# GpSimd adds the second norm's bias to the residual, and makes its dbx products two columns at a time

## The chip, the cores and the metric

The kernel runs on one core of one Trainium2 chip. The core has five engines with queues of their own: TensorE (PE) multiplies matrices into PSUM, VectorE (DVE) and ScalarE (ACT) do elementwise work, GpSimd (POOL) does elementwise work on SBUF, and SyncE (SP) issues the DMAs. The engines meet only at semaphores. The metric is device time of one launch in microseconds; lower is better.

## The reference, cut to what matters

The layer takes x of shape 4 x 2048 x 256 in f32. It is a Mamba block followed by an RWKV channel mix, each with a layernorm ahead of it and a residual around it:

```python
x = x + L0_attn_ref(layernorm(x), ...)
x = x + L0_ffn_ref(layernorm(x), ...)

# L0_attn_ref, N = 16 states for each of the 256 channels
dA  = exp(delta[..., None] * A)                  # b l d n
dBx = (delta * x)[..., None] * B_ssm[:, :, None] # b l d n
h   = dA_t * h + dBx_t                           # over l, for each d and n
y_t = sum over n of h[d, n] * C_t[n]
y   = y + x * D_param
res = (y * silu(z)) @ W_out + x_in
return (res - mean) * rsqrt(var + eps) * ln_g + ln_b
```

The sum that the channel mix starts from is therefore x + (normed res) * ln_g + ln_b. The term ln_b, a vector of 256 numbers that is the same for every token, is the bias that the change is about. The channel mix is r * ((relu(k) ^ 2) @ W_v^T), with r and k made from a mix of each token with the one before it.

## The kernel before, in words

The work is cut into 16 chunks of 512 tokens, four to a batch. A chunk of data with channels on the partitions is 2 halves x 512 tokens, that is 128 x 1024 numbers; with tokens on the partitions it is 4 blocks x 256 channels, also 128 x 1024.

For each chunk there are 16 columns, one per state n. A column takes these steps:

- ACT makes dA in PSUM, one activation per half (`exps`, line 662).
- POOL makes dbx = u * B_n in SBUF (`times_b`, line 543). u is delta * x of the chunk, B_n one row of the ring `b_ring`, spread over all partitions by a DMA. The result goes to the ring `dbx`, which has X_RING = 4 places.
- DVE runs the recurrence as a scan, one per half (`scans`, line 1045), into PSUM or into the ring `hg` of 8 places.
- The product with C_n, a row of the ring `c_ring`, is made either by DVE out of PSUM (the columns of SPLITS, lines 1052 and 1061) or by POOL in place in `hg` (the other, "whole" columns, `times_c`, line 556). Of the 16 columns, 8 or 9 are DVE's, by chunk parity; in the last chunk only 6.
- PE adds the product to y by transposes into PSUM (`add_up`, line 1331). This waits for POOL's product (semaphore g_pool) or DVE's (g_vec).

The order on each engine is written out by hand. A step t of the program has 16 places n (32 half-places on ACT and DVE). In place n, POOL makes the dbx product of column n + B_LEAD (3 before), then the C product of column n - C_LAG (1). PE adds up column n - Y_LAG (2). Tables such as PE_TURN and ACT_TURN say in which place each piece of dense work runs, so that step t works on the scan of chunk t, prepares chunk t + 1, and finishes chunks t - 1 (gate, W_out, second norm, residual) and t - 2 (channel mix). Each engine does its instructions strictly in this order, so one that waits holds up all that stand behind it.

The dbx product of column n waits for the scans of column n - 4, whose place it takes. `load_b` and `load_c` on SP fill the rings `b_ring` and `c_ring`, two groups of four rows each: a group is loaded once all products of the group two before it are made. SP's DMAs are in one queue too.

The second norm's result stands in a PSUM bank (`wo0`, `wo1`). DVE scales it (`affine`, line 1074). Then PE adds on top of it, in the loop `xa`, the residual `xres` by matmuls with the identity (line 1479) and the bias by transposes of `b_wide` (line 1485), where `b_wide` holds the bias of a channel in every column. ACT reads the bank back to `xres` with a running sum (`sum3`, line 880).

Of the kernel before, what the change touches and what calls it, by code (L numbers as in the profile page):

```python
# [5 lines left out]
P = 128  # L6
BATCH, LEN, D = 4, 2048, 256
NS = 16
LC = 512
# [8 lines left out]
X_RING = 4  # L18
# [6 lines left out]
B_LEAD, C_LAG, Y_LAG = 3, 1, 2  # L25
# [23 lines left out]
POOL_TURN = dict(nr1=13)  # L49
# [47 lines left out]
def mamba_rwkv_layer(nc, x_in, W_in, W_x, W_dt, b_dt, A_log, D_param, W_out, ln_g, ln_b,  # L97
# [12 lines left out]
    with ExitStack() as ctx:  # L110
# [6 lines left out]
        def sem(name):  # L117
# [22 lines left out]
        b_wide = sb("b_wide", P, KH, P)  # L140
# [66 lines left out]
            w_out_set b_set  # L207
# [157 lines left out]
        def c_of(n):  # L365
            return c_ring[:, n // GN % BG, n % GN:n % GN + 1, :]
# [48 lines left out]
        def _(sp):  # L415
# [33 lines left out]
            def step(t, par, pre=False, scan=False, mid=False, end=False, late=False, more=False):  # L449
# [3 lines left out]
                if scan:  # L453
                    if not (t == 0):
                        load_c(t, 1)
# [3 lines left out]
                if scan:  # L459
                    load_b(t, 2)  # L460
                    load_c(t, 2)
                    load_b(t, 3)
# [5 lines left out]
                if scan:  # L468
                    load_c(t, 3)
                if pre:  # L470
# [6 lines left out]
                    if start:  # L477
                        load_c(0, 1, True)
# [23 lines left out]
        def _(pool):  # L502
# [23 lines left out]
            def times_b(i, ip, n):  # L526
# [16 lines left out]
                pool.tensor_tensor(dbx[:, n % X_RING, :, :], u[:, ip, :, :], b.to_broadcast([P, KH, LC]),  # L543
                                   ALU.mult).then_inc(s["dbx_done"], 1)

            def times_c(i, n):

                need(pool, c_loaded[n // GN], 16 * (i + 1))
                if i == 0 and n == 0:
                    pool.wait_ge(s["w_loaded"], 16 * W_LOADS)  # L550
                if ends(i):
                    need(pool, s["scan_done"], KH * (NS * i + n + 1))
                else:
                    need(pool, s["carry_saved"], kept_wholes(i, n))
                part = hg[:, n % H_RING, :, :]
                pool.tensor_tensor(part, part, c_of(n).to_broadcast([P, KH, LC]), ALU.mult).then_inc(s["g_pool"], 1)  # L556
# [6 lines left out]
            def step(t, par, pre=False, scan=False, mid=False, end=False, late=False, more=False):  # L563
                nxt = 1 - par
                for n in range(NS):
                    if more and t >= 0 and n == POOL_TURN["nr1"]:
                        scale_mean(t + 3)
                    ahead = column_at(t, par, n + B_LEAD, scan, pre, mid)
                    if ahead:
                        times_b(*ahead)  # L570
                    behind = column_at(t, par, n - C_LAG, scan, pre, mid)
                    if behind and behind[2] in whole_of(behind[0]):
                        times_c(behind[0], behind[2])
                    if late and n == NS - 1:
                        for m in range(NS - C_LAG, NS - 1):
# [1049 lines left out]
```

## Time and profile before

| what | value |
|---|---|
| median of 3 runs | 941.3 us (941.04 to 941.36) |
| the profiled execution, its own time | 941.56 us |
| its span, first to last instruction | 939.8 us |
| mean granted TensorE clock | 0.978 |
| DVE busy | 900.5 us (96%) |
| POOL busy | 890.4 us (95%) |
| PE busy | 858.4 us (91%) |
| ACT busy | 837.5 us (89%) |

Some 1.8 us of the profiled execution lie outside the span. The busy shares are means over the whole span, which has a start of some 24 us and an end of some 27 us in which POOL has next to nothing to do. Busy times add up instruction durations as the profiler has them; two neighbours on POOL overlap there by some hundredths of a microsecond, so the distance from one start to the next is the better measure of what an instruction costs its engine.

### The profile page before, as it was taken

What the parts mean: (1) busy time and instruction counts of PE and PEld (TensorE: products, weight loads), DVE (VectorE), ACT (ScalarE), POOL (GpSimd) and SP (SyncE); (2) the same over time, 40 slices, a digit from 0 to 9 for tenths busy, and PEclk for the clock granted to TensorE, in tenths of its full rate; (3) what the DMA queues carried; (4) which work ended last, traced back from release to release, by engine and by line L of the source; (5) the groups of instructions that cost most, each with busy time, mean ns of one, the idle gap of its engine ahead of it and who ended that gap; (6) DMA issues with size and microseconds to landing.
All of it is one profiled execution on the core that took longest, in us unless ns stands there. A gap on an engine that the chain in (4) does not pass through costs nothing.

```text
span 939.8 us, 15796 instructions
## 1 busy us (share of the span) xinstructions
PE 858.4 (91%) x5024; PEld 685.0 (73%) x5024; DVE 900.5 (96%) x986; ACT 837.5 (89%) x2007; POOL 890.4 (95%) x413
## 2 busy tenths in 40 slices
PE   8766679989999898989999898998999899899998
PEld 5545466867878586776868678786878768678876
DVE  5899999999999999999999999999999999999896
ACT  4776889999999999998999999998999999978875
POOL 4999999999999999999999999999999999999980
PEclk9977899999999999999999999999999999999999
DMA  7345435462644644454374634446354454445231
GB/s 229 149 179 204 180 135 205 180 242 103 226 157 156 225 178 159 183 190 181 150 248 156 224 140 174 166 179 248 144 194 182 144 195 180 157 161 224 90 103 45
DMA packets 49939, 163.60 MB, mean 174 GB/s; under 512 B 5249, under 2 KB 33153, under 8 KB 33601
## 3 DMA queue, kind: packets, MB, share of 16 engines
q1 hardware_dynamic: 48528, 161.27, 46.0%
q0 software_dynamic: 512, 1.31, 0.5%
q8 instruction: 40, 0.66, 0.3%
q14 instruction: 43, 0.34, 0.1%
q10 hardware_dynamic: 816, 0.02, 0.1%
HBM read 153.15 MB, written 9.44 MB: 173 GB/s over the span
## 4 chain that ended last, share of the span: by engine, by line
PE 40%; ACT 27%; DVE 20%; issue 11%; POOL 1%; POOLq 0%; DVEq 0%; ACTq 0%
PE w_ps L1340 9%; ACT da_ps L662 9%; PE y_ps L1331 8%; DVE da_ps L1045 7%; PE w_ps L1364 5%; DVE hg L1045 4%; PE w_ps L1373 4%; PE w_ps L1376 4%; DVE hg L1052 4%; DVE hg L1061 3%; PE w_ps L1479 2%; ACT h_tok L599 2%; ACT zs L723 2%; PE w_ps L1382 2%; ACT xn_tok L599 2%
## 5 line engine op out<-in xcount | busy, mean ns | idle before, releaser
L543 POOL TENSOR_TENSOR dbx<-u,b_ring 128x1024 f32<-128x1024 f32 x255 | 599.7, 2379 | 2.0 <-DVE hg L1045 1.9
L662 ACT ACTIVATE da_ps<-delta,a_neg 128x512 f32<-128x512 f32 x512 | 340.2, 684 | 25.9 <-DVE hg L1052 8.6
L556 POOL TENSOR_TENSOR hg<-hg,c_ring 128x1024 f32<-128x1024 f32 x122 | 290.2, 2379 | 7.5 <-ACT carry L668 6.7
L1331 PE MATMUL y_ps<-ident,hg 128*128 128x128 f32 x2048 | 261.8, 278 | 10.4 <-POOL hg L556 10.2
L1331 PEld LDWEIGHTS y_ps<-ident,hg 128*128 128x128 f32 x2048 | 239.9, 144 | 37.4 <-issue 17.8
L1045 DVE TENSOR_TENSOR_SCAN da_ps<-da_ps,carry,dbx 128x512 f32<-128x512 f32 x203 | 249.5, 1270 | 3.5 <-ACT da_ps L662 3.5
L1045 DVE TENSOR_TENSOR_SCAN hg<-da_ps,carry,dbx 128x512 f32<-128x512 f32 x181 | 220.3, 1264 | 2.1 <-ACT carry L668 1.7
L1052 DVE TENSOR_TENSOR hg<-da_ps,c_ring 128x1024 f32<-128x1024 f32 x68 | 82.3, 1210 | 0.2
L1061 DVE TENSOR_TENSOR hg<-da_ps,c_ring 128x512 f32<-128x512 f32 x130 | 82.3, 673 | 0.0
L1045 DVE TENSOR_TENSOR_SCAN da_ps<-da_ps,dbx 128x512 f32<-128x512 f32 x64 | 75.4, 1211 | 3.4 <-ACT da_ps L662 3.1
L1045 DVE TENSOR_TENSOR_SCAN hg<-da_ps,dbx 128x512 f32<-128x512 f32 x64 | 74.8, 1206 | 2.4 <-ACT da_ps L662 2.4
L1340 PE MATMUL w_ps<-xnT_ring,w_in 128*128 128x512 f32 x120 | 61.7, 638 | 16.0 <-ACT xT L704 14.1
L1373 PE MATMUL w_ps<-w_rT,mixed 128*128 128x256 f32 x240 | 61.7, 380 | 0.0
L1376 PE MATMUL w_ps<-w_r_prev,mixed 128*128 128x256 f32 x240 | 61.6, 379 | 0.0
L1364 PE MATMUL w_ps<-w_in,xnT_ring 128*128 128x256 f32 x248 | 59.4, 382 | 0.9 <-ACT delta L696 0.6
L1340 PE MATMUL w_ps<-xnT_ring,w_dtx 128*128 128x512 f32 x120 | 57.9, 606 | 0.9 <-ACT bc_rows L808 0.9
L1364 PE MATMUL w_ps<-w_out,gated 128*128 128x256 f32 x248 | 58.7, 379 | 0.0
L1340 PE MATMUL w_ps<-mixed,w_kT 128*128 128x512 f32 x120 | 57.3, 601 | 0.0
L1364 PEld LDWEIGHTS w_ps<-w_in,xnT_ring 128*128 128x128 f32 x248 | 45.5, 190 | 15.0 <-ACT kact L690 4.9
L1373 PEld LDWEIGHTS w_ps<-w_rT,mixed 128*128 128x128 f32 x240 | 44.4, 190 | 11.4 <-issue 6.7
L1364 PE MATMUL w_ps<-w_vT,kact 128*128 128x256 f32 x232 | 52.6, 379 | 0.0
L1376 PEld LDWEIGHTS w_ps<-w_r_prev,mixed 128*128 128x128 f32 x240 | 45.6, 190 | 6.2
(214 smaller groups left out, 1320.7 us busy)
## 6 DMA issues: line engine op xcount, KB each, us to landing
c_ring<-bc_rows_dram SPq DMA_DIRECT2D x64, 1024.0 KB, 4.6
b_ring<-bc_rows_dram SPq DMA_DIRECT2D x63, 1024.0 KB, 6.6
xres<-in_L_attn_x_in_dram SPq DMA_DIRECT2D x16, 512.0 KB, 4.7
x_tok<-in_L_attn_x_in_dram SPq DMA_DIRECT2D x15, 512.0 KB, 6.0
out_dram<-r_out SPq DMA_DIRECT2D x14, 512.0 KB, 3.2
bc_rows_dram<-bc_rows SPq DMA_DIRECT2D x64, 16.0 KB, 5.4
w_in<-in_L_attn_W_in_dram SPq DMA_DIRECT2D x2, 256.0 KB, 4.3
x_tok<-in_L_attn_x_in_dram SPq DMA_DIRECT2D x2, 256.0 KB, 4.6
```

What stands on the lines that cost most here:

```text
L543: pool.tensor_tensor(dbx[:, n % X_RING, :, :], u[:, ip, :, :], b.to_broadcast([P, KH, LC]), ALU.mult).then_inc(s["dbx_done"], 1)
L556: pool.tensor_tensor(part, part, c_of(n).to_broadcast([P, KH, LC]), ALU.mult).then_inc(s["g_pool"], 1)
L599: last = act.activation(dst[j], src[j], ACT.Identity, scale=rs[j], bias=nm[j])
L662: act.activation(da_of(n, h), delta[:, ip, h, :], ACT.Exp, scale=a_neg[:, h, n:n + 1]).then_inc(s["da_ready"], 1)
L1045: dve.tensor_tensor_scan(out, da_of(n, h), dbx[:, n % X_RING, h, :], 0.0 if first else carry[:, n, h:h + 1], ALU.mult, ALU.add).then_inc(s ...
L1052: dve.tensor_tensor(hg[:, n % H_RING, :, :], da_both(n), c_of(n).to_broadcast([P, KH, LC]), ALU.mult).then_inc(s["g_vec"], 1)
L1061: last = dve.tensor_tensor(hg[:, n % H_RING, h:h + 1, :], da_ps[:, at:at + 1, :], c_of(n), ALU.mult)
L1331: last = pe.matmul(y_tok[:, b, h * P:(h + 1) * P], hg[:, n % H_RING, h, b * P:(b + 1) * P], ident[:, :], is_transpose=True, start=n == 0 a ...
L1340: last = pe.matmul(out, w[:, k, cols], x[:, k, :], start=k == 0, stop=k == KH - 1)
L1364: last = pe.matmul(by_block(out)[:, b, :], xT_[:, k, tokens], w[:, k, :], start=b == 0 and k == 0 and not begun, stop=k == KH - 1, skip_gr ...
L1373: pe.matmul(by_block(out)[:, b, :], h_of[:, k, at_b + 1:at_b + 1 + P], w_rT[:, k, :], start=k == 0, stop=False)
L1376: last = pe.matmul(by_block(out)[:, b, :], h_of[:, k, at_b:at_b + P], w_r_prev[:, k, :], start=False, stop=k == KH - 1)
```

## The change

POOL gets a new instruction, `add_bias`, once in each of the steps 1 to 15, ahead of the other work of place 5: it adds the bias (`b_all`, the bias on every partition) to `xres` in place, 128 x 1024 numbers. PE waits for this (`xb_done`) in place of the DMA, does only its identity matmuls, and no longer the transposes of `b_wide`; `b_wide` and the two activations that fill it are gone. In the last chunk the bias was and is added by DVE.

The dbx products of two neighbouring columns are made by one instruction (`times_b_twice`), in the even places, except the first two columns of the program. For that X_RING is 6, B_LEAD is 4, and a pair waits for the scans of the column that stood in the second of its two places. C products go on one by one (C_RUN = 1 makes every run one column long). On SP the loads of B stand ahead of the loads of C that used to be in front of them.

```diff
-X_RING = 4
+X_RING = 6
+C_RUN = 1
-B_LEAD, C_LAG, Y_LAG = 3, 1, 2
+B_LEAD, C_LAG, Y_LAG = 4, 1, 2
-POOL_TURN = dict(nr1=13)
+POOL_TURN = dict(xb=5, nr1=13)
...
         @block.sync
                 if scan:
+                    load_b(t, 2)
                     if not (t == 0):
                         load_c(t, 1)
...
                 if scan:
-                    load_b(t, 2)
+                    load_b(t, 3)
                     load_c(t, 2)
-                    load_b(t, 3)
...
-                if scan:
-                    load_c(t, 3)
                 if pre:
                     need(sp, s["bc_stored"], 16 * TB * (t + 2))
...
                     load_b(t + 1, 0, start)
+                if scan:
+                    load_c(t, 3)
+                if pre:
+                    if not start:
+                        load_b(t + 1, 1)
                     load_c(t + 1, 0, start)
-                    load_b(t + 1, 1, start)
...
         @block.gpsimd
+            def times_b_twice(i, ip, n):
+
+                need(pool, b_loaded[n // GN], 16 * (i + 1))
+                for m in range(KH):
+                    need(pool, s[f"u{m}_done"], i + 1)
+                need(pool, s["scan_done"], KH * (NS * i + n + 1 - X_RING + 1))
+                at, row = dbx_of(i, n), n % GN
+                b = b_ring[:, n // GN % BG, row:row + 2, :]
+                pool.tensor_tensor(dbx[:, at:at + 2, :, :], u[:, ip, :, :].unsqueeze(1).to_broadcast([P, 2, KH, LC]),
+                                   b.unsqueeze(2).to_broadcast([P, 2, KH, LC]), ALU.mult).then_inc(s["dbx_done"], 2)
...
+            def add_bias(t, nxt):
+
+                need(pool, s["xres_loaded"], 16 * t)
...
+                part = xres[:, nxt, :, :]
+                pool.tensor_tensor(part, part, b_all[:, :].unsqueeze(1).to_broadcast([P, TB, D]), ALU.add).then_inc(s["xb_done"], 1)
...
                 for n in range(NS):
+                    if mid and n == POOL_TURN["xb"]:
+                        add_bias(t, nxt)
...
-                    if ahead:
+                    if ahead and ahead[0] == 0 and ahead[2] < HEAD_COLS:
                         times_b(*ahead)
+                    elif ahead and ahead[2] % 2 == 0:
+                        times_b_twice(*ahead)
...
         @block.tensor
-                            need(pe, s["xres_loaded"], 16 * t)
+                            need(pe, s["xb_done"], t)
...
                             for j in range(2):
-                                pe.matmul(b[:, j, :], ident[:, :], xres[:, nxt, 2 * v + j, :], start=False, stop=False,
-                                          skip_group_check=True)
-                            if t == 1:
-                                pe.wait_ge(s["b_set"], KH)
-                            for j in range(2):
-                                for k in range(KH):
-                                    last = pe.matmul(b[:, j, k * P:(k + 1) * P], b_wide[:, k, :], ident[:, :],
-                                                     is_transpose=True, start=False, stop=True, skip_group_check=True)
+                                last = pe.matmul(b[:, j, :], ident[:, :], xres[:, nxt, 2 * v + j, :], start=False, stop=True,
+                                                 skip_group_check=True)
```

How the rows move on POOL in the last chunk, before. L543 is a dbx product, L556 a C product, L584 the half C product of the last column; the names in brackets are the semaphores waited for:

```order
L543 TENSOR_TENSOR dbx<-u,b_ring 128x1024 [waits u1_done,scan_done,u0_done,b_loaded2] x3
L556 TENSOR_TENSOR hg<-hg,c_ring 128x1024 [waits scan_done,c_loaded1]
L543 TENSOR_TENSOR dbx<-u,b_ring 128x1024 [waits u1_done,scan_done,u0_done,b_loaded3] x3
L556 TENSOR_TENSOR hg<-hg,c_ring 128x1024 [waits scan_done,c_loaded2]
L543 TENSOR_TENSOR dbx<-u,b_ring 128x1024 [waits u1_done,scan_done,u0_done,b_loaded3]
L556 TENSOR_TENSOR hg<-hg,c_ring 128x1024 [waits scan_done,c_loaded3] x2
L584 TENSOR_TENSOR hg<-hg,c_ring 128x512 [waits scan_done,c_loaded3]
```

And the same place now, where L572 is a pair of dbx products, L587 a C product, L596 the bias, L625 the half product:

```order
L596 TENSOR_TENSOR xres<-xres,b_all 128x1024 [waits xres_loaded]
L587 TENSOR_TENSOR hg<-hg,c_ring 128x1024 [waits scan_done,c_loaded1]
L572 TENSOR_TENSOR dbx<-u,b_ring 128x2048 [waits u1_done,u0_done,scan_done,b_loaded2]
L572 TENSOR_TENSOR dbx<-u,b_ring 128x2048 [waits u1_done,u0_done,scan_done,b_loaded3]
L587 TENSOR_TENSOR hg<-hg,c_ring 128x1024 [waits scan_done,c_loaded1]
L572 TENSOR_TENSOR dbx<-u,b_ring 128x2048 [waits u1_done,u0_done,scan_done,b_loaded3]
L587 TENSOR_TENSOR hg<-hg,c_ring 128x1024 [waits scan_done,c_loaded2]
L587 TENSOR_TENSOR hg<-hg,c_ring 128x1024 [waits scan_done,c_loaded3] x2
L625 TENSOR_TENSOR hg<-hg,c_ring 128x512 [waits scan_done,c_loaded3]
```

The last dbx products (columns 14 and 15) have moved ahead of the C product of column 10 (the one with c_loaded2), which had only the dbx product of column 15 behind it before.

On PE, a place of a middle step where the residual and the bias go on top of the second norm, before (L1331 is `add_up`, L1500 adds x * D to y):

```order
L1331 MATMUL y_ps<-ident,hg 128x128 x16
L1479 MATMUL w_ps<-xres,ident 128x256 x2
L1485 MATMUL w_ps<-ident,b_wide 128x128 x4
L1479 MATMUL w_ps<-xres,ident 128x256 x2
L1485 MATMUL w_ps<-ident,b_wide 128x128 x4
L1331 MATMUL y_ps<-ident,hg 128x128 x8
L1500 MATMUL y_ps<-ident,xT 128x128 x8
```

And now (L1368 is `add_up`, L1516 the residual, L1531 x * D):

```order
L1368 MATMUL y_ps<-ident,hg 128x128 x16
L1516 MATMUL w_ps<-xres,ident 128x256 x4
L1368 MATMUL y_ps<-ident,hg 128x128 x8
L1531 MATMUL y_ps<-ident,xT 128x128 x8
```

The eight transposes of a step are gone, and nothing else on PE has changed its place.

On SP, the DMAs of one middle step before, from the load of the residual to the store of the output:

```order
L452 DMA xres<-in_L_attn_x_in_dram 128x4x256
L446 DMA c_ring<-bc_rows_dram 128x2048 [waits g_pool,g_vec]
L458 DMA x_tok<-in_L_attn_x_in_dram 128x4x256 [waits xn_done]
L437 DMA b_ring<-bc_rows_dram 128x2048 [waits dbx_done]
L446 DMA c_ring<-bc_rows_dram 128x2048 [waits g_pool,g_vec]
L437 DMA b_ring<-bc_rows_dram 128x2048 [waits dbx_done]
L466 DMA bc_rows_dram<-bc_rows 32x128 [waits bc_rows_done]
L466 DMA bc_rows_dram<-bc_rows 32x128 x3
L446 DMA c_ring<-bc_rows_dram 128x2048 [waits g_pool,g_vec]
L437 DMA b_ring<-bc_rows_dram 128x2048 [waits dbx_done,bc_stored]
L446 DMA c_ring<-bc_rows_dram 128x2048 [waits g_pool,g_vec]
L437 DMA b_ring<-bc_rows_dram 128x2048 [waits dbx_done]
```

And now:

```order
L467 DMA xres<-in_L_attn_x_in_dram 128x4x256
L452 DMA b_ring<-bc_rows_dram 128x2048 [waits dbx_done]
L461 DMA c_ring<-bc_rows_dram 128x2048 [waits g_pool,g_vec]
L474 DMA x_tok<-in_L_attn_x_in_dram 128x4x256 [waits xn_done]
L452 DMA b_ring<-bc_rows_dram 128x2048 [waits dbx_done]
L461 DMA c_ring<-bc_rows_dram 128x2048 [waits g_pool,g_vec]
L481 DMA bc_rows_dram<-bc_rows 32x128 [waits bc_rows_done]
L481 DMA bc_rows_dram<-bc_rows 32x128 x3
L452 DMA b_ring<-bc_rows_dram 128x2048 [waits dbx_done,bc_stored]
L461 DMA c_ring<-bc_rows_dram 128x2048 [waits g_pool,g_vec]
L452 DMA b_ring<-bc_rows_dram 128x2048 [waits dbx_done]
L461 DMA c_ring<-bc_rows_dram 128x2048 [waits g_pool,g_vec]
```

Each B load now stands ahead of a C load that it stood behind.

## Rows read from the trace of the kernel before

**Rows 1.** The profile page, busy time by engine: us (share), instructions.

```profile
PE 858.4 (91%) x5024; PEld 685.0 (73%) x5024; DVE 900.5 (96%) x986; ACT 837.5 (89%) x2007; POOL 890.4 (95%) x413
```

**Rows 2.** The page, the chain that ended last, share by engine.

```profile
PE 40%; ACT 27%; DVE 20%; issue 11%; POOL 1%; POOLq 0%; DVEq 0%; ACTq 0%
```

**Rows 3.** Busy time by stretch: stretch, length, engines (instructions), clock, DMA.

```profile
400.00:460.00 60.00, 56.68 (x344) 45.56 (x343) 59.97 (x64) 55.94 (x135) 60.00 (x29) 1.00 0.52 193
520.00:580.00 60.00, 56.57 (x341) 45.45 (x340) 59.88 (x64) 56.93 (x141) 57.73 (x27) 1.00 0.45 168
40.00:880.00 840.00, 771.68 (x4562) 619.65 (x4562) 826.36 (x859) 772.20 (x1864) 831.30 (x372) 0.98 0.48 178
```

**Rows 4.** Waits of POOL: line, releaser, total us, times, longest.

```profile
POOL hg L556 <- ACT carry L668: 6.7, 9, 1.7
POOL dbx L543 <- DVE hg L1045: 1.9, 3, 0.9
POOL hg L556 <- DVE hg L1045: 0.8, 1, 0.8
```

**Rows 5.** Waits of DVE and of PE, in the same form.

```profile
DVE da_ps L1045 <- ACT da_ps L662: 6.6, 11, 1.4
DVE da_ps L1045 <- POOL dbx L541: 0.3, 1, 0.3
...
PE w_ps L1382 <- ACT xn_tok L599: 28.9, 14, 2.6
```

**Rows 6.** POOL's groups by shape: busy us, mean ns, idle before.

```profile
L543 POOL TENSOR_TENSOR dbx<-u,b_ring 128x1024 f32<-128x1024 f32 x255 | 599.7, 2379 | 2.0 <-DVE hg L1045 1.9
L556 POOL TENSOR_TENSOR hg<-hg,c_ring 128x1024 f32<-128x1024 f32 x122 | 290.2, 2379 | 7.5 <-ACT carry L668 6.7 <-DVE hg L1045 0.8
L561 POOL TENSOR_TENSOR nr<-nm,rs 128x4 f32<-128x4 f32 x14 | 3.0, 217 | 0.0
L584 POOL TENSOR_TENSOR hg<-hg,c_ring 128x512 f32<-128x512 f32 x1 | 1.3, 1272 | 0.0
```

**Rows 7.** POOL in order of time, the first products: start, us.

```profile
23.31 1.26 POOL L541 TENSOR_TENSOR dbx<-u,b_ring 128x512 f32<-128x512 f32 x1 [0.90 <-DVE u L1082]
24.54 11.63 POOL L543 TENSOR_TENSOR dbx<-u,b_ring 128x1024 f32<-128x1024 f32 x5
36.10 2.37 POOL L556 TENSOR_TENSOR hg<-hg,c_ring 128x1024 f32<-128x1024 f32 x1
```

**Rows 8.** POOL in order of time, the last products.

```profile
901.18 2.38 POOL L556 TENSOR_TENSOR hg<-hg,c_ring 128x1024 f32<-128x1024 f32 x1
903.50 2.38 POOL L543 TENSOR_TENSOR dbx<-u,b_ring 128x1024 f32<-128x1024 f32 x1
906.69 4.71 POOL L556 TENSOR_TENSOR hg<-hg,c_ring 128x1024 f32<-128x1024 f32 x2 [0.81 <-DVE hg L1045]
911.36 1.27 POOL L584 TENSOR_TENSOR hg<-hg,c_ring 128x512 f32<-128x512 f32 x1
```

**Rows 9.** PE in order of time, the same stretch.

```profile
904.15 1.04 PE L1331 MATMUL y_ps<-ident,hg 128*128 128x128 f32 x8
905.02 1.03 PE L1373 MATMUL w_ps<-w_rT,mixed 128*128 128x256 f32 x4
...
908.48 2.78 PE L1331 MATMUL y_ps<-ident,hg 128*128 128x128 f32 x24
911.10 0.60 PE L1357 MATMUL da_ps<-ident,xnT_ring 128*128 128x128 f32 x4
911.53 1.04 PE L1331 MATMUL y_ps<-ident,hg 128*128 128x128 f32 x8
912.77 1.06 PE L1331 MATMUL y_ps<-ident,hg 128*128 128x128 f32 x8 [0.21 <-POOL hg L584]
```

**Rows 10.** The chain from 340 to 400 us: start, us, piece.

```profile
345.80 0.44 PE w_ps L1485 x4
```

**Rows 11.** DMA issues: size of one, median us to landing.

```profile
c_ring<-bc_rows_dram SPq DMA_DIRECT2D x64, 1024.0 KB, 4.6
b_ring<-bc_rows_dram SPq DMA_DIRECT2D x63, 1024.0 KB, 6.6
```

More of the change, by code:

```diff
@@ L363, in column_at, with c_of, dbx_of, products_of @@
             return (t, par, n) if scan else None
-        def c_of(n):
-            return c_ring[:, n // GN % BG, n % GN:n % GN + 1, :]
+        def c_of(n, k=1):
+            return c_ring[:, n // GN % BG, n % GN:n % GN + k, :]
+        def dbx_of(i, n):
+            return (NS * i + n) % X_RING
+        def products_of(i):
+            runs = []
+            for n in whole_of(i):
+                if i == LAST and n == NS - 1:
+                    break
+                if runs and len(runs[-1]) < C_RUN and runs[-1][-1] == n - 1 and n % GN:
+                    runs[-1].append(n)
+                else:
+                    runs.append([n])
+            return runs
         def da_of(n, h):
@@ L542, in times_b, with times_c @@
                     return
-                pool.tensor_tensor(dbx[:, n % X_RING, :, :], u[:, ip, :, :], b.to_broadcast([P, KH, LC]),
+                pool.tensor_tensor(dbx[:, dbx_of(i, n), :, :], u[:, ip, :, :], b.to_broadcast([P, KH, LC]),
                                    ALU.mult).then_inc(s["dbx_done"], 1)
-            def times_c(i, n):
+            def times_b_twice(i, ip, n):
[7 more added lines that the diff above has]
+                                   b.unsqueeze(2).to_broadcast([P, 2, KH, LC]), ALU.mult).then_inc(s["dbx_done"], 2)
+            def times_c(i, run):
+                n, k = run[0], len(run)
                 need(pool, c_loaded[n // GN], 16 * (i + 1))
@@ L551, in times_c @@
                 if ends(i):
[L552 removed]
+                    need(pool, s["scan_done"], KH * (NS * i + run[-1] + 1))
                 else:
[L554 to L556 removed]
+                    need(pool, s["carry_saved"], kept_wholes(i, run[-1]))
+                slot = n % H_RING
+                part = hg[:, slot:slot + k, :, :]
+                pool.tensor_tensor(part, part, c_of(n, k).unsqueeze(2).to_broadcast([P, k, KH, LC]),
+                                   ALU.mult).then_inc(s["g_pool"], k)
+            def add_bias(t, nxt):
+                need(pool, s["xres_loaded"], 16 * t)
+                if t == 1:
+                    pool.wait_ge(s["w_loaded"], 16 * W_LOADS)
+                part = xres[:, nxt, :, :]
+                pool.tensor_tensor(part, part, b_all[:, :].unsqueeze(1).to_broadcast([P, TB, D]), ALU.add).then_inc(s["xb_done"], 1)
             def scale_mean(count):
@@ L568, in step @@
                     ahead = column_at(t, par, n + B_LEAD, scan, pre, mid)
-                    if ahead:
+                    if ahead and ahead[0] == 0 and ahead[2] < HEAD_COLS:
                         times_b(*ahead)
+                    elif ahead and ahead[2] % 2 == 0:
+                        times_b_twice(*ahead)
                     behind = column_at(t, par, n - C_LAG, scan, pre, mid)
[L572 to L575, printed above, removed]
-                            if m in whole_of(t):
-                                times_c(t, m)
+                    for run in products_of(behind[0]) if behind else []:
+                        if behind[2] == run[-1]:
+                            times_c(behind[0], run)
             def close():
@@ L766, in step @@
                         act.wait_ge(s["w_loaded"], 16 * W_LOADS)
-                        act.wait_ge(s["ident_done"], 1)
-                        for k in range(KH):
-                            act.activation(b_wide[:, k, :], ident[:, :], ACT.Identity, scale=0.0,
-                                           bias=b_col[:, k:k + 1]).then_inc(s["b_set"], 1)
                     if t == 0 and place == 6:
@@ L1199, in second @@
                     part = xres[:, par, 2 * v:2 * v + 2, :]
-                    dve.wait_ge(s["xb_done"], 1)
+                    dve.wait_ge(s["xb_done"], NT)
                     dve.wait_ge(last_g[v], 1)
```

7 lines of the change are left out of this document (3 added, 4 removed).

## The prediction

> **What bounds the kernel now.** I began with the busy times of the page. DVE stands at 900.5 us and POOL at 890.4 us of a span of 939.8 us, with PE and ACT behind at 858.4 and 837.5 [rows 1]. Shares of a whole span hide its start and end, so I read the busy time by stretches next. From 40 to 880 us POOL is busy 831.3 of 840 us and DVE 826.4; PE and ACT have 68 us of air each. Between 400 and 460 us both POOL and DVE are full, 60.0 and 59.97 of 60 us [rows 3]. So two engines run at their own speed, and neither has room for more than a few microseconds.
>
> The waits say which one gives way. POOL's three waits in the loop sum to 6.7 + 1.9 + 0.8 = 9.4 us, for the carries that ACT saves after a scan and for DVE's scans themselves [rows 4]. DVE never waits for a dbx product after the first column (0.3 us there); it waits for ACT's dA, 6.6 us [rows 5]. POOL is thus a hair faster than DVE, by some 1%, and hardly anything waits for it.
>
> The chain that ended last seems to say something else: PE 40%, POOL 1% [rows 2]. I do not take it as a price list. Where four engines are this full, each step of the chain could as well have gone through a neighbour that was just as late.
>
> **The measure of POOL.** Durations of neighbours on POOL overlap slightly, so I use distances of starts. POOL runs without a break but for those 9.4 us from 24.54 us to 911.36 + 1.27 = 912.63 us [rows 7, 8], 888.1 us, of which 878.7 are work. Less the half product (1.3) and 14 small ones (0.15 each, 2.1, my estimate from what is left of 217 ns once neighbours overlap), the other 254 + 1 + 122 = 377 instructions of 128x1024 [rows 6] take 875.3 us, 2.32 us each.
>
> **Part 1, the bias on POOL.** 15 instructions of 128x1024, one per step 1 to 15, two SBUF inputs and written in place, as the C product is (2379 ns, line 556, against 2379 ns for dbx, so the operation and the place do not show) [rows 6]. 15 x 2.32 = +34.8 us on POOL. It waits only for the residual, whose DMA is issued at the head of the step, five places before.
>
> **Part 2, pairs.** 255 dbx instructions become 1 + 127 of 128x2048. The trace shows none of that length. From the 512 and 1024 sizes: the first start at 23.31 to the next at 24.54 is 1.23 us, and the five that follow take (36.10 - 24.54)/5 = 2.31 us each [rows 7]. A straight line gives a fixed part of 2 x 1.23 - 2.31 = 0.15 us, and a pair saves one fixed part. By durations in the full loop, 2379 against 1272 ns [rows 6], it is 2 x 1272 - 2379 = 165 ns of duration, of which some 0.06 is overlap of neighbours (2.38 less 2.32) and not a saving: 0.11 us. I take the middle, 0.13: a pair costs 4.51 us. 127 x 0.13 = -16.5 us; the ends are 0.11 (-14.0) and 0.15 (-19). If pairs with two broadcast inputs save nothing, the term is 0; that they save more than 0.20 no row supports, but none excludes it.
>
> The Trainium skill ("GPSIMD Engine Reference", section Performance versus the Vector engine) gives 4497 ns for a tensor_tensor add of 2048 f32 elements on GpSimd. Taken as it is and with the same overlap of 0.06, a pair would save 2 x 2.32 - 4.44 = 0.20 us, 25 us in all, and by that rule the sum below would be some 9 us lower, about 945. No row here shows a 2048, so I leave this outside the sum; it is a rival below for the case that pairs are that cheap.
>
> POOL's net: +34.8 - 16.5 = **+18.3 us** of work on an engine that has 9.4 us of waits to fill. The new work per chunk is 34.8/15 - 16.5/16 = +1.3 us; POOL becomes the slowest engine and DVE the one that waits.
>
> Do the 9.4 us vanish? They come when POOL is level with DVE. A POOL that needs 1.3 us more per chunk falls behind DVE, and then carries and scans are ready when it asks. The ring of six lets it run four columns ahead, and a pair asks for the scan of the column just passed, as a single one did. What limits this is the boundary of a chunk: the C product of column 15 now stands behind the pair 4, 5, PE adds it up ahead of its transposes for the channel mix, and DVE waits for these between its columns 2 and 4. By my reckoning of the orders, DVE can meet both this and the ring with some 3 us to spare. I let 1.0 us of POOL's waits stay: -9.4 + 1.0 = **-8.4 us**, with 0 and 9.4 as the ends of what may remain.
>
> **Part 3, PE.** 15 x 8 transposes go, 0.44 us for four [rows 10]: 15 x 0.88 = 13.2 us. PE has 68 us of air in the loop [rows 3], and after the change waits for POOL's products. I count **0**; ACT's read of the bank comes a little earlier and has nothing urgent behind it. If POOL were not the bound, this could be worth something (a rival).
>
> **Part 4, the end.** All that follows the last product is as before, so I shift it by POOL's end E, but for one queue. Before, POOL made the C product of column 10 at 901.18 to 903.56, 9.1 us ahead of its end at 912.63 [rows 8]. Now the dbx product of column 15 no longer stands behind it: after it come only 13, 14 and the half, so it ends at E - 1.27 - 2 x 2.32 = E - 5.9. PE reached the sum of column 10 at 904.15, that is E - 8.5, and had after it 3.46 us of the late r, three sums (2.62), a residual (0.43), a sum, and then the last sum at 912.77 = E + 0.14 [rows 9]. From E - 5.9: 0.87 + 3.46 + 2.62 + 0.43 + 0.87 = 8.25, so the last sum starts at E + 2.35, **+2.2 us**. The ends are 0, should the order of late work loosen elsewhere, and 4, should DVE end late too.
>
> **Part 5, SP and the start.** C loads now stand behind B loads; a C load takes 4.6 us to land and a B load 6.6 [rows 11]. A B load waits for products that POOL makes four or more columns ahead, so what is put behind it is held little. In the first chunk the pair 2, 3 is ready 2.2 us later than column 2 was; DVE waits, POOL does not. Two activations of ACT go. **0** for all of this, with a bound of 2 us up for a C load that holds DVE's product of column 12 in some chunks, where I see the least slack.
>
> **The sum.** Against the execution's own 941.56 us (span 939.8 and 1.8 outside): +18.3 - 8.4 + 2.2 = +12.1, 953.7 us. The median of the runs is 0.3 lower, which gives **953.4 us**. The ends of this case are 950 (saving 0.15, no waits left, 1 at the end) and 958 (saving 0.11, 4 of waits left).
>
> **Rivals.**
>
> *The waits of POOL stay* (12%). POOL's waits are with carries and scans at fixed places, and if DVE, held by PE at each chunk boundary, is late there, POOL waits again. Then nothing of 9.4 is given back: 941.3 + 18.3 + 2.2 = 962, or 959 with part of it. For it speaks that POOL and DVE are within 1% of each other [rows 3], against it that DVE's work is 5 us less than POOL's even now.
>
> *Pairs cost more than two singles* (7%). The instruction has four dimensions and both inputs repeat. With a saving of 0: 34.8 - 8.4 + 2.2 = 28.6 up, 970. Against it: the single already repeats B over the two halves at the pace of the C product, which does too.
>
> *Pairs are as cheap as 0.20 saved* (10%). 34.8 - 25.4 = 9.4, which POOL's waits just absorb: 941.3 + 9.4 - 8.4 + 2.2 = 944.5, still slower by over 0.2%.
>
> *Not slower: the fixed cost of a POOL instruction with its four waits is larger than the slope shows* (12% in all). Place: the dbx products of all chunks. If a pair saves 0.34 (4.30 us), 43 us go, POOL's work falls by 8.4, DVE becomes the bound again, and the 0.9 us that PE no longer spends per chunk show where DVE waits for it: some 938 to 941. It decides from a saving of 0.22 on (25.4 + 2.2 us over 127). Removed work of PE is on the chain [rows 2, 10], and a reader who prices by the chain would say 941.3 - 13.2 = 928; the 68 us of air on PE and its 28.9 us of waiting for ACT's xn_tok [rows 5] speak against it.
>
> **How the numbers follow.** Forecast 59%, the rivals 12, 7, 10 and 12%. A difference of 0.2%, 1.9 us, is what a measurement here can tell. The last rival splits into 7% faster and 5% same, and a part of the cheap pairs falls within 0.2%: 2%. So faster 0.07, same 0.07, slower 0.86. The range for 8 in 10 takes in the cheap pairs and the waits that stay: 944 to 961. The likeliest case's own is 950 to 958.
>
> **What would show it.** POOL busy 908 or more, in one stretch without breaks from 24.5 us to some 922; the 128x2048 product near 4.57 us of duration; DVE with new waits for dbx of 15 to 25 us in all; PE busy 845 or so with more waiting for POOL's hg; the gap from POOL's last product to the end 29 us where it was 27. Wrong would be: POOL's waits at 9 us or more, pairs under 4.45 us, or a DVE without waits for dbx.

## The result, and the profile after

The changed kernel takes **952.9 us** (median of 3 runs, 952.89 to 953.16) against 941.3, a ratio of 1.0125 with a 95% interval of 1.0102 to 1.0148. It is slower by 11.6 us; 953.4 were forecast. The profiled execution has a span of 951.1 us against 939.8, so 11.3 of the 11.6 us are in the trace.

The page's busy times after, which answer to [rows 1], and below them the shares of the chain that ended last, which answer to [rows 2]:

```profile
PE 852.6 (90%) x4904; PEld 675.5 (71%) x4904; DVE 900.4 (95%) x986; ACT 835.9 (88%) x2005; POOL 906.3 (95%) x301
...
DVE 30%; ACT 26%; PE 19%; issue 17%; POOL 6%; DVEq 0%; POOLq 0%; ACTq 0%
```

POOL has 15.9 us more to do. The chain now gives PE 19% where it gave 40%, and POOL only 6% (1% before), although POOL is the engine that sets the pace. Two kernels that differ by 1% have quite different chains: it is no price list here.

The busy time by stretch after (stretch, length, then PE, PE loads, DVE, ACT and POOL with their counts, the clock, the DMA), for [rows 3]:

```profile
400.00:460.00 60.00, 56.60 (x322) 44.82 (x320) 59.39 (x62) 54.86 (x135) 60.00 (x20) 0.97 0.55 193
...
40.00:880.00 840.00, 754.73 (x4381) 601.36 (x4380) 818.83 (x850) 762.93 (x1845) 840.00 (x264) 0.97 0.50 178
```

POOL is busy 840.0 of 840 us, where it had 8.7 us of air. DVE has dropped from 826.4 to 818.8: it waits now. The waits of POOL, DVE and PE after (line, releaser: total us, times, longest), for [rows 4, 5]:

```profile
POOL hg L587 <- DVE hg L1082: 5.0, 1, 5.0
```
```profile
DVE da_ps L1082 <- ACT da_ps L703: 11.3, 10, 4.4
DVE mixed L1135 <- ACT mixed L759: 10.0, 8, 3.0
...
DVE da_ps L1082 <- POOL dbx L572: 0.6, 1, 0.6
```
```profile
PE y_ps L1368 <- POOL hg L587: 32.7, 15, 8.6
```

In the loop POOL never waits. But DVE hardly waits for POOL's dbx (0.6 us). The chain goes round: PE waits for POOL's C products, 32.7 us in all (10.2 before); ACT waits for PE, 12.0 us for `mixed` alone (3.0 before); and DVE waits for ACT, 21 us in the two rows shown, of which the first was 6.6 before [rows 5] and the second 2.5.

POOL's groups by shape after (busy us, mean ns), for [rows 6], and POOL in order of time at the start and at the end, for [rows 7, 8]:

```profile
L572 POOL TENSOR_TENSOR dbx<-u,b_ring 128x2048 f32<-128x2048 f32 x127 | 584.4, 4621 | 0.0
L587 POOL TENSOR_TENSOR hg<-hg,c_ring 128x1024 f32<-128x1024 f32 x122 | 296.1, 2446 | 5.0 <-DVE hg L1082 5.0
L596 POOL TENSOR_TENSOR xres<-xres,b_all 128x1024 f32<-128x1024 f32 x15 | 36.8, 2450 | 0.0
```
```profile
24.44 2.35 POOL L561 TENSOR_TENSOR dbx<-u,b_ring 128x1024 f32<-128x1024 f32 x1
26.75 13.51 POOL L572 TENSOR_TENSOR dbx<-u,b_ring 128x2048 f32<-128x2048 f32 x3
40.20 2.36 POOL L587 TENSOR_TENSOR hg<-hg,c_ring 128x1024 f32<-128x1024 f32 x1
...
894.63 9.23 POOL L572 TENSOR_TENSOR dbx<-u,b_ring 128x2048 f32<-128x2048 f32 x2
903.64 2.54 POOL L587 TENSOR_TENSOR hg<-hg,c_ring 128x1024 f32<-128x1024 f32 x1
905.95 4.74 POOL L572 TENSOR_TENSOR dbx<-u,b_ring 128x2048 f32<-128x2048 f32 x1
910.45 2.55 POOL L587 TENSOR_TENSOR hg<-hg,c_ring 128x1024 f32<-128x1024 f32 x1
917.99 4.72 POOL L587 TENSOR_TENSOR hg<-hg,c_ring 128x1024 f32<-128x1024 f32 x2 [4.99 <-DVE hg L1082]
922.67 1.28 POOL L625 TENSOR_TENSOR hg<-hg,c_ring 128x512 f32<-128x512 f32 x1
```

By distance of starts a pair costs (40.20 - 26.75)/3 = 4.48 us early and (903.64 - 894.63)/2 = 4.51 late. Over all 127 pairs the mean distance is 4.494 us, and over the single products before (those with no wait behind them) it is 2.320. The mean duration, 4621 ns, is longer than that: it holds the overlap with the next instruction, which has grown to 0.1 and 0.2 us (the C product at 903.64 is stamped 2.54 us long, and the next starts 2.31 us after it). Who subtracts durations would read a C product as dearer than before, 2446 against 2379 ns, and it is not. Waits are counted from the stamped end, so they come out short by the same overlap: by starts the wait of 4.99 us is 917.99 - 910.45 - 2.32 = 5.2 us.

POOL's stretch, from the first whole dbx product to the end of the half product, is 24.44 to 923.95, 899.5 us, where it was 888.1. From 923.95 to the end of the span it is 27.2 us, as before. So all of the difference lies in this stretch, and I use it to compare kernels below; it leaves out the start, which differs by 2 us between executions.

### The profile page after: what moved, and what is told of

Its sections match the earlier page's. It is cut to its first block, busy times and chain, and to the rows that moved or that the text cites. A ratio compares the mean times of both kernels' runs of the same rounds, so it can differ in the third digit from the quotient of the medians.

```text
span 951.1 us, 15191 instructions
## 1 busy us (share of the span) xinstructions
PE 852.6 (90%) x4904; PEld 675.5 (71%) x4904; DVE 900.4 (95%) x986; ACT 835.9 (88%) x2005; POOL 906.3 (95%) x301
## 4 chain that ended last, share of the span: by engine, by line
DVE 30%; ACT 26%; PE 19%; issue 17%; POOL 6%; DVEq 0%; POOLq 0%; ACTq 0%
DVE da_ps L1082 13%; ACT da_ps L703 11%; DVE hg L1082 6%; PE w_ps L1377 6%; DVE hg L1089 5%; PE y_ps L1368 3%; POOL hg L587 3%; DVE hg L1098 3%; POOL dbx L572 2%; PE w_ps L1401 2%; ACT spare L654 2%; PE w_ps L1410 1%; PE w_ps L1413 1%; ACT h_tok L640 1%; ACT spare L646 1%
## 5 line engine op out<-in xcount | busy, mean ns | idle before, releaser
L572 POOL TENSOR_TENSOR dbx<-u,b_ring 128x2048 f32<-128x2048 f32 x127 | 584.4, 4621 | 0.0
L587 POOL TENSOR_TENSOR hg<-hg,c_ring 128x1024 f32<-128x1024 f32 x122 | 296.1, 2446 | 5.0 <-DVE hg L1082 5.0
L1368 PE MATMUL y_ps<-ident,hg 128*128 128x128 f32 x2048 | 264.4, 279 | 33.0 <-POOL hg L587 32.7
L1368 PEld LDWEIGHTS y_ps<-ident,hg 128*128 128x128 f32 x2048 | 239.9, 144 | 64.0 <-POOL hg L587 37.6
L1377 PE MATMUL w_ps<-xnT_ring,w_dtx 128*128 128x512 f32 x120 | 59.9, 624 | 0.8 <-ACT bc_rows L845 0.8
L1410 PEld LDWEIGHTS w_ps<-w_rT,mixed 128*128 128x128 f32 x240 | 45.0, 193 | 11.6 <-issue 6.7
```

Source lines behind the costliest of these rows:

```text
L572: pool.tensor_tensor(dbx[:, at:at + 2, :, :], u[:, ip, :, :].unsqueeze(1).to_broadcast([P, 2, KH, LC]), b.unsqueeze(2).to_broadcast([P, 2, ...
L587: pool.tensor_tensor(part, part, c_of(n, k).unsqueeze(2).to_broadcast([P, k, KH, LC]), ALU.mult).then_inc(s["g_pool"], k)
L1368: last = pe.matmul(y_tok[:, b, h * P:(h + 1) * P], hg[:, n % H_RING, h, b * P:(b + 1) * P], ident[:, :], is_transpose=True, start=n == 0 a ...
L1377: last = pe.matmul(out, w[:, k, cols], x[:, k, :], start=k == 0, stop=k == KH - 1)
L1410: pe.matmul(by_block(out)[:, b, :], h_of[:, k, at_b + 1:at_b + 1 + P], w_rT[:, k, :], start=k == 0, stop=False)
```

## The experiments

The theory after the result: POOL's work sets the time, and its waits are what gives way first. The rivals: the new order on the engines costs, PE's work counts, the loads count.

**One part alone: the bias on POOL, dbx products single.** On the kernel before:

```diff
-POOL_TURN = dict(nr1=13)
+POOL_TURN = dict(xb=5, nr1=13)
+                    if mid and n == POOL_TURN["xb"]:
+                        add_bias(t, nxt)
-                            need(pe, s["xres_loaded"], 16 * t)
+                            need(pe, s["xb_done"], t)
-   (PE's transposes of b_wide)
...   (add_bias itself, as in the change)
```

> One part alone: the bias goes from PE to POOL in steps 1 to 15, the dbx products stay single (X_RING 4, B_LEAD 3, loads in the order of before). Theory (the amount of POOL's work sets the time): 15 x 2.32 = 34.8 us more on POOL, of which at most its 9.4 us of waits are absorbed, so +25.4 to +31 us, 967 to 972 us, POOL without breaks between 24.5 us and the last chunk. Rival (the change is slow because C products stand behind pairs and the lead of 4 disturbs PE, not because of the work): this kernel has none of that and should stay within 5 us of 941.

966.9 us (before on the same chip 941.6), ratio 1.0255 (1.0234 to 1.0275), +25.3 us. The last rows of POOL, with the only wait that it has from its first whole product on:

```profile
931.40 4.72 POOL L555 TENSOR_TENSOR hg<-hg,c_ring 128x1024 f32<-128x1024 f32 x2 [0.47 <-DVE hg L1050]
936.07 1.28 POOL L593 TENSOR_TENSOR hg<-hg,c_ring 128x512 f32<-128x512 f32 x1
```

The stretch starts at 24.35 us here and is 913.0 us long: 33.8 us more work, and the 9.4 us of waits down to 0.5. That is the 15 x 2.32, with nearly all of the waits absorbed; the time is at the lower end of what was expected. The rival, that the order makes the loss, is out as the main cause.

**The other part alone: pairs, lead of 4, new order of loads, bias on PE.**

```diff
-POOL_TURN = dict(xb=5, nr1=13)
+POOL_TURN = dict(nr1=13)
-                    if mid and n == POOL_TURN["xb"]:
-                        add_bias(t, nxt)
+   (b_wide and PE's transposes as before the change)
...
```

> The other part alone: pairs of dbx products, X_RING 6, B_LEAD 4 and the new order of loads, while PE keeps the bias transposes. Theory: POOL's work falls by 127 x 0.15 = 19 us to some 860 us, POOL waits for DVE about 28 us, DVE is the bound, and the time is 938 to 942. Rival (the new order itself costs): the C products behind the pairs hold PE, then ACT, then DVE, and the time is 944 to 950 although POOL has less to do.

945.3 us, ratio 1.0029 (1.0016 to 1.0042). POOL's waits:

```profile
POOL dbx L573 <- DVE hg L1085: 22.9, 22, 3.2
...
POOL hg L588 <- DVE hg L1085: 6.5, 1, 6.5
POOL dbx L573 <- DVE da_ps L1085: 0.6, 1, 0.6
```

POOL's work fell to 861.8 us (stretch 891.8 less 30.0), and its waits grew to 30 as expected, but the time lies in the rival's range. DVE is the bound, and something in the new order holds it: 3.7 us in the stretch against before. What it is, the run with C products first shows further down.

**No bias at all in chunks 0 to 14.**

```diff
-                    if mid and n == POOL_TURN["xb"]:
-                        add_bias(t, nxt)
-                            need(pe, s["xb_done"], t)
+                            need(pe, s["xres_loaded"], 16 * t)
...
```

This kernel leaves ln_b out of the results of those chunks; it is there for its time alone.

> The changed kernel with the bias of chunks 0 to 14 left out altogether (neither POOL's add nor PE's transposes; ln_b is missing from those chunks' results). Against the pairs alone it differs by PE's 120 transposes, 13.2 us of PE work. Theory: PE has air, so within 2 us of the pairs alone, 937 to 941. Rival (PE is the clock of the loop, as its 40% of the chain before suggests): up to 13 us lower than the pairs alone, about 928.

942.9 us, ratio 1.0008 (0.9992 to 1.0024). It is above the 937 to 941 expected, since the pairs alone are too. It is 2.4 us under the pairs alone, but the two profiled executions differ by 2.3 us in when POOL begins; by the stretch it is 1.3 us (890.5 against 891.8). So PE's 13.2 us are worth 1 or 2 us at best. Against the changed kernel, POOL's 15 instructions are worth 10 us (9.0 by the stretch).

**The changed kernel with the old order of loads.**

```diff
                 if scan:
-                    load_b(t, 2)
                     if not (t == 0):
                         load_c(t, 1)
...
-                    load_b(t, 3)
+                    load_b(t, 2)
                     load_c(t, 2)
+                    load_b(t, 3)
...   (and load_c(t, 3) ahead of the loads of chunk t + 1)
```

> The changed kernel with the DMA queue's order of before (C loads ahead of B loads). Theory: the loads have slack either way, within 1 us of the changed kernel, 952 to 954. Rival (the new order of loads costs, or is needed by the pairs): more than 2 us off in either direction, a B load landing after POOL wants it would show as POOL waiting for a DMA.

989.9 us, ratio 1.0501 (1.0477 to 1.0525): 37 us slower than with the new order (35.4 by the stretch). My theory was far off. POOL's waits, and one of them in order of time with the DMA queue:

```profile
POOL dbx L569 <- issue: 24.4, 10, 3.5
...
POOL dbx L569 <- ACT carry L706: 8.9, 4, 2.4
POOL hg L584 <- DVE hg L1079: 4.8, 1, 4.8
POOL dbx L569 <- DMA b_ring<-bc_rows_dram: 1.6, 1, 1.6
```
```profile
441.34 0.33 SPq L461 DMA_DIRECT2D c_ring<-bc_rows_dram  x1
441.73 0.43 SPq L473 DMA_DIRECT2D x_tok<-in_L_attn_x_in_dram  x1
442.21 0.50 SPq L452 DMA_DIRECT2D b_ring<-bc_rows_dram  x1
```
```profile
441.17 4.58 POOL L569 TENSOR_TENSOR dbx<-u,b_ring 128x2048 f32<-128x2048 f32 x1
445.65 2.43 POOL L584 TENSOR_TENSOR hg<-hg,c_ring 128x1024 f32<-128x1024 f32 x1
450.17 4.53 POOL L569 TENSOR_TENSOR dbx<-u,b_ring 128x2048 f32<-128x2048 f32 x1 [2.09 <-issue]
```

The C load at 441.34 waits for POOL's C product of column 15 of the chunk before, which is made after the pair 4, 5 and ends as POOL begins the next pair at 441.17. The B load of columns 8 to 11 stands two DMAs behind it, is issued at 442.21, and POOL wants it one pair and one C product later. It waits. The rows name the releaser of most of these waits "issue" or a carry; that they are waits for the load I read from this order, and the next run bears it out.

**Only one of the loads moved back to the new order.**

```diff
                 if scan:
+                    load_b(t, 2)
                     if not (t == 0):
                         load_c(t, 1)
...
-                    load_b(t, 2)
                     load_c(t, 2)
                     load_b(t, 3)
```

> The kernel with the old order of loads (989.9 us) with one of its moves made: the B load of group 2 stands ahead of the C load of group 1, all else as in the old order. Theory: the 37 us come from this load alone, which in the old order stands behind a C load that waits for POOL's product of column 15, made after the pair 4, 5, and so lands after POOL wants it for the pair 8, 9: 952 to 957. Rival (the later loads count too, in particular the B load of the next chunk's group 1 behind a C load): 965 to 985.

955.2 us, ratio 1.0144 (1.0131 to 1.0157). One DMA carries 35 of the 37 us, and the 33 us of waits named "issue" and carry are gone with it; what is left is 2.4 us of POOL waiting for `b_ring`.

**C products ahead of the pairs.** The changed kernel's last chunk was the next question: POOL waits 5.0 us there, where I had forecast 1. In its trace, for PE, ACT and DVE (start, us, and in brackets the wait before):

```profile
872.03 1.28 PE L1368 MATMUL y_ps<-ident,hg 128*128 128x128 f32 x8 [3.42 <-POOL hg L587]
...
880.68 1.03 PE L1413 MATMUL w_ps<-w_r_prev,mixed 128*128 128x256 f32 x4
```
```profile
881.75 0.60 ACT L772 ACTIVATE r_out<-w_ps 128x512 f32<-128x512 f32 x1 [2.80 <-PE w_ps L1413]
882.36 1.28 ACT L860 ACT_TABLE_LOAD   x1
883.66 0.69 ACT L703 ACTIVATE da_ps<-delta,a_neg 128x512 f32<-128x512 f32 x1
```
```profile
884.38 1.29 DVE L1082 TENSOR_TENSOR_SCAN da_ps<-da_ps,carry,dbx 128x512 f32<-128x512 f32 x1 [4.43 <-ACT da_ps L703]
```

PE waits for the C product of column 15, then makes r; ACT's tanh waits for r, its dA stands behind the tanh, and DVE's scan comes 4.4 us late. The edit:

```diff
+                    behind = column_at(t, par, n - C_LAG, scan, pre, mid)
+                    for run in products_of(behind[0]) if behind else []:
+                        if behind[2] == run[-1]:
+                            times_c(behind[0], run)
                     ahead = column_at(t, par, n + B_LEAD, scan, pre, mid)
...   (the pairs, as they were)
-                    behind = column_at(t, par, n - C_LAG, scan, pre, mid)
-   (and its three lines)
```

> The changed kernel with one thing in another order: in each place POOL makes the C product ahead of the pair of dbx products, so the C product of column 15 no longer stands behind the pair 4, 5. Theory: the 5.0 us that POOL waits at the end are the answer of a chain that POOL itself starts in the last chunk (C product of column 15 late, PE waits 3.4 us for it, then its r matmuls, ACT's tanh, ACT's dA, DVE's scan 4.4 us late). With C first PE gets that product 4.5 us earlier, most of the 5.0 us vanish and the time is 948 to 950. Rival (DVE is simply the slower engine in the last chunk): unchanged, 952 to 954.

952.9 us, ratio 1.0121 (1.0106 to 1.0135): no gain where 948 to 950 was expected. The stretch is 899.5 us again, with a wait of 4.9 at its end. The scan's wait fell from 4.4 to 1.7 us, PE's waits for C products from 32.7 to 11.7, and in their place stood a new pair, PE for the bias and DVE for PE:

```profile
892.50 3.38 PE L1516 MATMUL w_ps<-xres,ident 128*128 128x256 f32 x8 [4.73 <-POOL xres L596]
```
```profile
899.77 0.70 DVE L1144 SCALAR_TENSOR_TENSOR w_ps<-r_out,w_ps 128x512 f32<-128x512 f32 x1 [5.94 <-PE w_ps L1401]
```

**The bias early in the last step, with C first, and alone.**

```diff
-POOL_TURN = dict(xb=5, nr1=13)
+POOL_TURN = dict(xb=5, xb_late=3, nr1=13)
-                    if mid and n == POOL_TURN["xb"]:
+                    if mid and n == POOL_TURN["xb_late" if late else "xb"]:
```

> The changed kernel with C products ahead of the pairs and, in the last step only, the bias in place 3 of POOL's order in place of 5 (some 9 us earlier). Theory: with C first, PE's wait for column 15 no longer made the end late, but PE then waited 4.7 us for the bias itself in the last step, where it wants it three places earlier than in other steps, and DVE 5.9 us for PE; one wait took the other's place. With both gone POOL's 5.0 us at the end shrink to under 2 and the time is 948 to 950. Rival (the last chunk is bound by DVE whatever is done): 952 to 954.

> The changed kernel with the bias early in the last step alone, pairs ahead of C products as in the changed kernel. Theory: here the late C product of column 15 still holds PE, ACT and DVE (the 4.4 us), so this alone brings nothing: 952 to 954, POOL's wait at the end 4 to 5 us. Rival (the bias was the cause from the start): 948 to 950, as with both.

951.5 us, ratio 1.0099 (1.0082 to 1.0116), with both, and 955.1, ratio 1.0133 (1.0116 to 1.0149), with the bias alone. Neither is what its theory wanted (948 to 950, and 952 to 954). The stretches are 899.1 and 899.5 us, the waits at the end 4.4 and 4.9. PE no longer waits for the bias in either; with both, what DVE waits for in the last chunk is, among others, the pair itself:

```profile
894.66 2.46 DVE L1082 TENSOR_TENSOR_SCAN da_ps<-da_ps,carry,dbx 128x512 f32<-128x512 f32 x2 [2.44 <-POOL dbx L572]
```

So the wait-by-wait theory of the last chunk is wrong as a price. POOL arrives there late in all four orders, the engines in the ring are late behind it, and from the scans that wait for the pair above on DVE still needs some 25 us to its scans of column 13 (894.66 to 919.45 in that execution), where POOL has only 20 us of products (three pairs and three C products). What is left is 4.4 to 5.0 us in four orders of the same work, or 4.9 to 5.2 us by distances of starts.

The kernel with the bias alone, whose wait there is only 0.5 us, shows what the pairs have to do with it. DVE's scan is late in it too:

```profile
897.79 1.29 DVE L1050 TENSOR_TENSOR_SCAN da_ps<-da_ps,carry,dbx 128x512 f32<-128x512 f32 x1 [4.93 <-ACT da_ps L671]
```

From this scan to the end of the scans of column 13 DVE takes 33.6 us there (897.79 to 931.40) and 33.6 us in the changed kernel (884.38 to 917.99). But POOL has some 39 us of work left at that scan with single products and a lead of three, and some 34.5 us with pairs and a lead of four: it is about one pair further ahead, and that gains nothing. That this handover is the cause I read from the traces; no run here made DVE's part of it shorter, and none set the lead back alone.

**C first with the pairs alone, and then work moved from DVE to POOL.** The first is the pairs-alone kernel with the same edit as above. The second sets, on top of it, column 3 of chunks 1, 5, 9 and 13 as whole:

```diff
-SPLITS = [[0, 2, 5, 6, 8, 11, 12, 14], [0, 2, 3, 5, 6, 8, 11, 12, 14]]
+SPLITS = [[0, 2, 5, 6, 8, 11, 12, 14], [0, 2, 5, 6, 8, 11, 12, 14], [0, 2, 5, 6, 8, 11, 12, 14], [0, 2, 3, 5, 6, 8, 11, 12, 14]]
-            return LAST_SPLIT if i == LAST else SPLITS[i % 2]
+            return LAST_SPLIT if i == LAST else SPLITS[i % len(SPLITS)]
```

> The pairs alone (bias on PE) with C products ahead of the pairs. Theory: here POOL waited 6.5 us at the end for the same chain; without it the time is that of DVE's own pace, 939 to 942, no slower than before. Rival (pairs as such hold DVE): 944 to 946 as the pairs alone.

> The kernel of the pairs with C first, bias on PE, and four C products (column 3 of chunks 1, 5, 9 and 13) moved from DVE to POOL. Theory: the pairs free 19 us of POOL, of which 4 x 2.32 = 9.3 are spent; DVE sheds 4 x 1.2 = 4.8 us and is the bound, so 935 to 938, faster than both. Rival (what DVE sheds goes into waits for PE and ACT at chunk boundaries): within 1 us of the kernel without the move.

942.3 us, ratio 1.0006 (0.9997 to 1.0015), and 938.9, ratio 0.9964 (0.9951 to 0.9977). Here C first did help: the pairs alone hardly cost any more (942.3 us against an upper end of 942), and the stretch went from 891.8 to 888.3 us, that of before. The wait at POOL's end fell from 6.5 to 2.9 us, which is all of the difference. With DVE as the bound a late C product costs time; with POOL as the bound the same edit brought nothing. The four columns moved are worth 3.5 us by the medians and 5.3 by the stretch (888.3 to 883.1), where 4.8 were reckoned. The twelve runs of that kernel spread from 935.9 to 941.0 us, and the profiled one is among the shortest, so neither figure is good to a microsecond. Its 938.9 us are above the 935 to 938 expected.

The same for all chunks but the last, by `SPLITS = [[0, 2, 5, 6, 8, 11, 12, 14]]`:

> The rebalanced kernel (938.9 us) with column 3 of chunks 3, 7 and 11 moved to POOL as well, so that each chunk but the last has 8 whole columns. Theory: POOL still has 12.6 us of waits in the rebalanced kernel and takes 7.0 of them, DVE sheds 3.6 us more: 935 to 938. Rival (POOL and DVE are level by then, and what is shed is lost at the chunk boundaries): 938 to 941.

**933.9 us, ratio 0.9919 (0.9904 to 0.9934)**, faster than both kernels and than the 935 to 938 expected: 8.1 us under before on the same chip. Its busy times and POOL's waits:

```profile
PE 858.1 (92%) x5024; PEld 686.9 (74%) x5024; DVE 892.8 (96%) x979; ACT 837.6 (90%) x2003; POOL 888.4 (95%) x293
```
```profile
POOL hg L588 <- DVE hg L1085: 2.9, 1, 2.9
...
POOL hg L588 <- ACT carry L708: 0.7, 2, 0.4
```

POOL is full again, but with C products that DVE sheds. Seven columns take 7 x 1.2 = 8.4 us off DVE by my estimate (1.2 us is one such product on DVE; its busy time fell by 7.7), and the time fell by 8.1.

The profiled executions side by side; work is the stretch less the waits shown in it:

| kernel | POOL's stretch, us | waits | work | median, us (before in its job) |
|---|---|---|---|---|
| before | 888.1 | 9.4 | 878.7 | 941.3 |
| changed | 899.5 | 5.0 | 894.5 | 952.9 (941.3) |
| bias on POOL alone | 913.0 | 0.5 | 912.5 | 966.9 (941.6) |
| pairs alone | 891.8 | 30.0 | 861.8 | 945.3 (941.6) |
| no bias | 890.5 | 28.7 | 861.8 | 942.9 (941.6) |
| old loads | 934.9 | 39.7 | 895.2 | 989.9 (941.6) |
| old loads, one moved | 902.1 | 7.4 | 894.7 | 955.2 (941.5) |
| changed, C first | 899.5 | 4.9 | 894.6 | 952.9 (941.5) |
| the same, bias early | 899.1 | 4.4 | 894.7 | 951.5 (942.0) |
| changed, bias early | 899.5 | 4.9 | 894.6 | 955.1 (942.0) |
| pairs, C first | 888.3 | 27.1 | 861.2 | 942.3 (941.5) |
| the same, four columns moved | 883.1 | 12.6 | 870.5 | 938.9 (941.5) |
| all but last chunk with 8 | 880.3 | 3.6 | 876.7 | 933.9 (942.0) |

The work column adds up: pairs take 16.9 us away, the bias adds 32.7 to 33.8. The time does not: bias alone +25.3, pairs alone +3.7, both +11.6. What 17 us less work is worth depends on who is the bound: with the bias on PE nothing, with the bias on POOL 14 us (966.9 to 952.9).

## Why the prediction was right

- **What bounds it.** Right. The full POOL, with 9.4 us of waits, was the engine that could not take more; the kernel with the bias alone, without a break to the last chunk, shows it.
- **The bias, +34.8.** Right: +33.8 in the kernel with the bias alone, and 15 x 2.33 = 34.9 by the distances of starts in the changed kernel. The traces count a wait from the end of the stamped duration, so that each wait is some 0.06 us too short and the work of before, with 13 waits, up to 0.8 us too high; that is the size of the difference.
- **The pairs, -16.5.** Right in kind, 2 us too small. By distances of starts a pair saves 2 x 2.320 - 4.494 = 0.146 us, all of them 18.5 us, near the end of 0.15 that the prediction named; by the table's work, which is blurred by the counting of waits, it is 16.9. The Trainium skill's 4497 ns ("GPSIMD Engine Reference", section Performance versus the Vector engine) agrees with that distance of starts; the stamped durations here run from 4494 to 4737 ns, with a median of 4617. The prediction had taken an overlap of 0.06 off the Trainium skill's figure. That was the error in its 0.20 us: left whole, the figure gives 2 x 2.32 - 4.497 = 0.14 us, an estimate.
- **The sum on POOL, +18.3.** 15.8 was measured, by the trace's own waits, and some 16.4 by distances of starts (34.9 less 18.5). So 2 of the 2.5 us too much are the pairs, and the rest is the counting of waits.
- **The waits, -8.4.** Mis-sized: -4.4. All waits in the loop went, as argued, but 5.0 us came back as one wait in the last chunk. I had taken 1.0 there.
- **The end, +2.2.** This step failed. I had worked out that PE's late sum of column 10 would start the last sum late. In the trace PE reaches that sum at 915.80, after the product is done, and the last part from POOL's end to the span's end is 27.2 us, as before. DVE's lateness in the last chunk, which the prediction had only as a reason for the upper end of 4, came first and hid the queue: POOL stood 5 us between the product of column 10 and the next. 1.0 + 2.2 = 3.2 us were forecast for what is now 5.0 + 0.
- **PE at 0.** Right within 1 or 2 us, by the kernel without bias.
- **Loads at 0.** Right for the change as made, for a reason I did not see: I priced the move of the B loads, but not what it prevents. With pairs and the old order the cost is 37 us. The sentence that a B load waits for products made four columns ahead was true of its semaphore and false of its place in the queue.
- **What would show it.** POOL busy 906.3 where I wanted 908 or more, PE 852.6 where 845 was named; no breaks in the loop, as said, but one of 5.0 us behind it. The 120 transposes are gone from PE's count, yet its busy time fell by 5.8 us and not by 13.2: other matmuls took longer, the sums of products 264.4 us where they took 261.8, at a granted clock of 0.969 against 0.978. That DVE would wait 15 to 25 us for dbx was wrong, and "a DVE without waits for dbx" stood among the signs of being wrong. It waits 0.6 us for dbx and some 21 us through POOL's C products, PE and ACT. So POOL is the bound as said, but what carries its pace to DVE is the C product and not dbx.
- **The ends, 950 and 958.** They do not come out of their own terms: 34.8 - 19 - 9.4 + 1 = +7.4 gives 949, and 34.8 - 14.0 - 5.4 + 2.2 = +17.6 gives 959. The measured time lies within either pair.

The errors of +2.5, -4.0 and +2.2 nearly cancel (measured less forecast in the span: 11.3 against 12.1, 0.1 of it from an earlier start). That is luck: the number is better than the argument was, and what the argument had right is the bound and the size of the two terms of work.

## What to carry to other kernels

Where two engines are full, price a change by the work of the engine that cannot take it, less the waits that it has to give, and measure work on GpSimd by distances of starts. The shares of the chain are no prices there: they changed from PE 40% to 19% for a 1% change of time. Merged instructions gain time only if what they free is filled: with the bias on PE, 17 us of freed GpSimd time were worth nothing until products moved over from VectorE, and with the bias on GpSimd they were worth 14. When a producer's order changes, walk through every DMA that stands in the same queue behind one that waits for it.

## What the runs showed of the hardware

- A GpSimd product of 128x2048 f32 costs 4.48 to 4.51 us from start to start, one of 128x1024 2.31 to 2.33 and one of 128x512 1.23; the fixed part, from any two of these sizes, is 0.13 to 0.15 us. The pattern (inputs repeated over two or over four blocks, mult or add, in place or not) moved a 128x1024 by 0.01 us at most.
- The stamped durations of these instructions can grow along a run while the distances stay: in the changed kernel a 128x1024 is 2.36 us long at 40 us and 2.54 at 904 us, each with the next start 2.31 to 2.32 us later. Behind a wait they are short again: after the one of 5.0 us the next C product is stamped 2.37 us, and in the kernel with C first and the bias early, the most drawn out, 2.86 us ahead of the last wait and 2.36 behind it. How they grow differs between executions: with the bias alone they reach 2.53 us on the way and stand at 2.41 at 926 us, with no wait between, so a wait is not all that sets them back.
- The start differs by some 2 us between executions of near relatives: the first whole dbx product begins at 24.0 to 24.6 us in ten of the profiled executions and at 26.3 to 26.5 in three. That makes differences under 2 us between medians unsafe, and is why the stretch is compared above. It is not the only spread: the runs of the kernel with four columns moved differ by 5.0 us, and no trace here shows why.
